# Mixing and convolution products cut from half-array to eighth-array tiles

## The reference, cut to what matters

```python
# layer 0: a 64x64 mixing matrix for each batch
agg_w = jnp.einsum('bk,koi->boi', att, weight[..., 0])
out = jnp.einsum('boi,bih->boh', agg_w, x) + agg_b[:, :, None]
# layer 1: a grouped convolution, 9 taps, 4 groups of 16 channels
out = lax.conv_general_dilated(x, weight, window_strides=(STRIDE,), padding=[(PAD, PAD)],
                               dimension_numbers=('NCH', 'OIH', 'NCH'), feature_group_count=GROUPS)
# behind both: base linear map 1024 -> 1024, and a gated low-rank part of 8 experts, rank 16
```

## Time and profile before

| | |
|---|---|
| time, median of 3 runs | 2087.89 us (2087.43 to 2088.1) |
| time of the profiled execution | 2088.04 us |
| span of the profiled execution | 2086.2 us |
| instructions in the trace | 61022 |
| granted TensorE clock, mean | 1.00 |
| PE matmuls and weight loads | 22221 of each |

### The profile page before, as it was taken

The page is one execution under the profiler, slowest core; times in us unless marked ns, Lnnn a source line. Parts: engine busy times, 40 slices in busy tenths (PEclk is TensorE's granted clock), DMA queues, the critical chain, the costliest instruction groups (busy, mean ns, idle before and its releaser), DMA issues.

```text
span 2086.2 us, 61022 instructions
## 1 busy us (share of the span) xinstructions
PE 2077.8 (100%) x22221; PEld 1979.4 (95%) x22221; DVE 1531.9 (73%) x5264; ACT 314.3 (15%) x941; POOL 966.9 (46%) x1318
## 2 busy tenths in 40 slices
PE   9999999999999999999999999999999999999999
PEld 8999999999999999999999999999999999999998
DVE  6766766667667666666788887777778888877776
ACT  4211111111111111111211111111111111111110
POOL 3644444444444444444854444444444454544442
PEclk9999999999999999999999999999999999999999
DMA  6434334343343343344433343333333333333332
GB/s 244 137 96 115 106 104 112 98 110 110 94 114 106 101 115 98 109 111 116 128 95 104 107 104 94 94 94 94 94 101 104 103 100 94 94 94 94 98 104 80
DMA packets 152180, 222.76 MB, mean 107 GB/s; under 512 B 18256, under 2 KB 100176, under 8 KB 152144
## 3 DMA queue, kind: packets, MB, share of 16 engines
q1 hardware_dynamic: 151808, 221.97, 38.9%
q10 hardware_dynamic: 336, 0.30, 0.1%
HBM read 121.47 MB, written 100.73 MB: 107 GB/s over the span
## 4 chain that ended last, share of the span: by engine, by line
PE 99%; DVE 0%; DMA 0%; ACT 0%; issue 0%; DVEq 0%; ACTq 0%
PE psB L1083 79%; PE psB L1109 8%; PE psT L1061 7%; PE psT L1024 3%; PE psB L1183 1%; DMA outb<-in_condw 0%; PE psT L1039 0%; PE psT L1117 0%; DVE Wlo L769 0%; DVE Ylo L755 0%; PE psB L1117 0%; DVE outb L804 0%; ACT Whi L572 0%; DVE Y L725 0%; DVE outb L797 0%
## 5 line engine op out<-in xcount | busy, mean ns | idle before, releaser
L1083 PE MATMUL psB<-Whi,Yhi 128*128 128x384 f32 x3024 | 723.2, 346 | 1.6 <-DVE outb L804 1.4
L1083 PE MATMUL psB<-Wlo,Yhi 128*128 128x384 f32 x3024 | 703.3, 340 | 0.0
L1083 PE MATMUL psB<-Whi,Ylo 128*128 128x384 f32 x3024 | 701.1, 339 | 0.0
L1083 PEld LDWEIGHTS psB<-Whi,Yhi 128*128 128x128 f32 x3024 | 537.7, 189 | 26.6 <-issue 2.2
L1083 PEld LDWEIGHTS psB<-Whi,Ylo 128*128 128x128 f32 x3024 | 549.8, 189 | 0.0
L1083 PEld LDWEIGHTS psB<-Wlo,Yhi 128*128 128x128 f32 x3024 | 548.6, 188 | 0.1
L442 POOL TENSOR_TENSOR res<-res,bias 128x256 f32<-128x256 f32 x256 | 180.0, 734 | 541.1 <-DMA res<-x_scratch 541.1
L917 DVE STREAM_TRANSPOSE HT<-hw 32x32 f32<-32x32 f32 x1968 | 397.5, 202 | 25.1
L471 POOL TENSOR_TENSOR Ylo<-Y,Yhi 128x256 fp32r<-128x256 f32 x244 | 190.7, 801 | 322.2 <-ACT Yhi L546 322.2
L432 POOL TENSOR_TENSOR res<-Xraw,bias 128x256 f32<-128x256 f32 x248 | 218.2, 913 | 206.0 <-DVE outb L804 195.3
L804 DVE TENSOR_TENSOR outb<-psB,res 128x384 f32<-128x384 f32 x381 | 223.6, 673 | 122.4 <-PE psB L1109 122.4
(11 more groups left out here) (132 smaller groups left out, 1578.4 us busy)
## 6 DMA issues: line engine op xcount, KB each, us to landing
x_scratch<-outb SPq DMA_DIRECT2D x64, 512.0 KB, 2.7
x_block_scratch<-outb SPq DMA_DIRECT2D x512, 64.0 KB, 1.9
Xraw<-x_block_scratch SPq DMA_DIRECT2D x128, 256.0 KB, 5.1
res<-x_scratch SPq DMA_DIRECT2D x64, 512.0 KB, 4.7
out<-outb SPq DMA_DIRECT2D x64, 512.0 KB, 2.9
Xraw<-in_x SPq DMA_DIRECT2D x62, 512.0 KB, 3.4
row<-row_scratch SPq DMA_DIRECT2D x126, 64.0 KB, 4.2
stage<-in_l0w SPq DMA_DIRECT2D x8, 580.5 KB, 12.8
```

The costliest lines, as they stand in the source:

```text
L1083: last = mm(psB[:, 3 * par + b, 0:cols], y, w[:, k, BANK0[b]:BANK0[b] + cols], start=(k == 0 and y is yh and w is Whi), stop=(k == KT - 1 ...
```

## The change

Each of the products is cut in two: the stationary operand is now 64 rows by 32 columns, its result goes to 32 partitions of psT, and `tile_position` names the eighth of the array (half the rows, a quarter of the columns) on which it stands. A round over m and a is eight products instead of four. The moving operand stays 64 by 64. A burst has 64 products, and since each is still two weight loads and two matmuls, 256 instructions instead of 128. SQ is 32.

```diff
@@ -1015,15 +1015,15 @@
-            def mix_squares(j, par):
+            def mix_eighths(j, par):
 
                 half = slice(0, C), slice(C, P)
                 for k in range(KT):
-                    for m in range(2):
+                    for m in range(0, P, SQ):
                         for a in range(2):
-                            last = mm(psT[half[m], a, k * C:(k + 1) * C],
-                                      x_tile(j, par)[half[a], k * P + m * C:k * P + (m + 1) * C],
-                                      M[half[a], half[a]], start=True, stop=True)
+                            last = mm(psT[m:m + SQ, a, k * C:(k + 1) * C],
+                                      x_tile(j, par)[half[a], k * P + m:k * P + m + SQ],
+                                      M[half[a], half[a]], start=True, stop=True, tile_position=(a * C, m))
                 last.then_inc(mixed, NC)
@@ -1055,11 +1055,11 @@
                 half = slice(0, C), slice(C, P)
                 for k in range(2):
                     for w in range(PRODUCTS):
-                        for m in range(2):
+                        for m in range(0, P, SQ):
                             for a in range(2):
                                 to = (k * PRODUCTS + w) * C
-                                last = mm(psT[half[m], a, to:to + C], Xs[half[a], w, 2 * i + k, half[m]],
-                                          CT[half[a], k, w, :], start=True, stop=True)
+                                last = mm(psT[m:m + SQ, a, to:to + C], Xs[half[a], w, 2 * i + k, m:m + SQ],
+                                          CT[half[a], k, w, :], start=True, stop=True, tile_position=(a * C, m))
                 last.then_inc(mixed, 2)
```

More of the change, by code:

```diff
@@ L1246, in step @@
                     if lay1 == 0 and k == MIX_AFTER:
-                        mix_squares(*after(j, par))
+                        mix_eighths(*after(j, par))
                     if lay1 == 1 and k in conv_after:
```

## The result

The kernel before took 2087.99 us (median of 4 runs, 2087.43 to 2088.89), the changed one 2152.85 (4 runs, 2151.16 to 2154.2): a ratio of 1.0309, 95% interval 1.0296 to 1.0322. I had forecast 2113, range 2086 to 2185, so the direction and the range held, but the change is 65 us where the forecast has 25.

A forecast was written before the change was run, and what follows sets the result against it. The prediction took TensorE, busy all the time, to bound the kernel. Instruction supply would add 0.133 us to each of 189 bursts, 25 us on 2088.04, giving 2113 us, range 2086 to 2185.

The forecast's parts named there:

- no gain on the array: In a burst, moving columns set the 58 ns round, so cutting the stationary operand saves no array time; sum 0.
- The exit of a burst: Entering and leaving a burst costs TensorE some time, claimed to be the same before and after the change.
- the supply of instructions becomes the bound: In bursts, the sequencer at 4.7 ns an instruction can't follow the array's 3.6; +0.133 us a burst, 25 us; chance 0.48.
- 223 instructions x 4.7, and some 0.03, that is 1.08: Burst from first weight load to last matmul: 256 instructions less 33 queued, at 4.7 ns each; 1.08 us against 0.945.
- 8 ns lag: Sequencer's delay in a burst, 30 ns against 22 in the slow stretch, read as supply of 4.7 ns an instruction.
- rival C: Bursts much slower: 7.3 ns is the sequencer's pace (+135 us) or an empty queue costs more (+95 us); chance 0.18.
- rival D: TensorE's code is loaded again in layer 1's loop, all 30 rounds; 2140 to 2300 us, chance 0.10.
- nothing else moved: Behind the bursts, VectorE's load per tile and its 0.8 us distance stay, and DMAs are as before.
- Rivals A and B: Sequencer needs 4.2 ns or less. A: no change, 2088, chance 0.17. B: shorter first weight load stays, 2083, chance 0.07.

The follow-up runs named there:

- half-array run: Against the kernel before: 16 products a burst over half the rows and all 128 columns, two side by side, 64 instructions; 2245.15 us.
- the quarters' run: The kernel before with two waits, long satisfied, put in the middle of each burst; 2088.12 us, ratio 1.0002.

## Why the prediction was right in direction and wrong in size

**Right: no gain on the array.** Moving columns set the round of the kernel before, with the weights close behind, and cutting the weights brought nothing back. The wide and the half-array run show both sides of it. The exit of a burst stays as it was (144 ns from last matmul to next weight load, 147 before).

**Right, in part: the supply of instructions becomes the bound.** Wide moving operands, with half the instructions, make 0.89 us of 1.268; the queue is found with 11 instructions ahead instead of 37 in the middle of a burst; pieces that are short against the queue's content run at full pace.

**Wrong: the term "223 instructions x 4.7, and some 0.03, that is 1.08".** It measured 1.268, so +0.323 us a burst and not +0.133. Three things in it:

- The pace. In the change it is one matmul in 10.04 ns from the 34th on (94 in 0.944 us), stops and all, where the forecast has 9.4. The even stretches are faster. I had read 4.7 ns an instruction out of an 8 ns lag, and the even stretches show 4.17 (8.33 a pair). The lag was of the right size for a wrong reason, or mixed with one. Taken alone this term was too long: 223 x 4.17 = 0.93.
- The start of supply. I let it begin with the burst, from a queue with 33 ahead. In the trace 66 instructions go at full pace, and then there is a hole: the 34th matmul starts 84 ns after the 32nd, and with 16 moving columns, where the array can't be the cause, 96 ns after it (0.164 to 0.260 us). The depth of the queue wasn't 33 everywhere, either: 37 in the quarters' run.
- The stops. In the even part a weight load comes late each 34 pairs, with 64 moving columns, and not with 16 or 32: from the 69th load to the 103rd it takes 329 ns, where 34 pairs at 8.33 are 283. The runs give 1.085, 1.098 and 1.268 us for 16, 32 and 64 columns, and 1.213 for 64 with half the weights. So of the 0.323 us a burst, 0.140 are there with 16 columns, and 0.183 only with 64: 0.064 ahead of the 34th matmul (0.324 against 0.260 us), where the array's rounds set the pace, and 0.119 behind it (94 steps in 0.944 us against 0.825). The 0.119 are a price that only shows with matmuls of full length and a queue near empty, and part of it is weight loads that aren't covered any more.

By the forecast's own line, 0.03 us and then 9.4 ns a pair, the 34th matmul is due at 0.20 us. It came at 0.324. So the beginning makes some 0.13 of the missing 0.19 us, and the 94 steps behind it the other 0.06.

The price of an empty queue was in my rival C ("an empty queue costs more than supply"), with +95 us and a chance of less than 0.18. What took place is between the forecast and this rival, which I had treated as an alternative though it is a consequence: once supply is the bound the queue is empty, and then what the queue hid comes out. That 2152.85 lies in the range is partly luck: the range went above 2137 for rival C, whose sum I didn't use, and for rival D, which didn't happen.

**Right: nothing else moved.** No wait for VectorE, DMAs as before. **Rival D fell:** ten more pieces of code were loaded, once; the loop of 1,352 instructions isn't loaded again in its 30 rounds. Rivals A and B would have needed 4.2 ns an instruction or less. The pace did come out at 4.17, and they didn't come true, because of the hole and the stops: their condition was stated for the wrong quantity.

**What stays open** is what makes the hole behind the 66th instruction and the stops each 34 pairs. The runs exclude the order of tiles, the count of columns on the array, tiles of 32 columns as such, and the place in the program (it is the same in all 189 bursts). The hole goes by count and not by time: it is ahead of the 34th weight load with 16, 32, 64 and 128 moving columns, where the load before stands at 0.134, 0.134, 0.195 and 0.355 us, though with 128 only 17 ns of it are left. It needs eight tiles in use: four at a time take instructions at the same 7 ns each as the wide operands, and don't have it. The regular stops came with 64 moving columns and not with 16 or 32. Each f32 product is two passes on one tile, which for eight tiles makes 32 instructions to fill them all, about the queue's content; whether the second passes clog the queue I only argue, and no run shows it.

## What to carry to other kernels

Before cutting a product into more tiles, ask which of its two lengths sets the round on the array, the moving columns or the weights; cutting the other one only adds instructions. Then divide the burst's time by its instructions: with 7.3 ns each this kernel's TensorE was safe, with 3.6 ns each it wasn't, and pieces of 64 instructions ran at full pace in any case, from a queue with some 33 ahead. And when a sum shows that a queue will run empty, price also what the full queue hid, weight loads ahead of their matmuls for one.

## What the runs showed of the hardware

- TensorE took up instructions in an even 8.33 ns for a weight load and a matmul when nothing else bound it (16 moving columns, 64 pairs in 0.533 us). Out of the queue, at a burst's start, it took 31 such pairs in 0.162 us.
- A round on the tiles takes 56 ns with 16 or 32 stationary columns, 58 with 64, 112 with 128, for 64 moving columns of f32.
- Matmuls on different tiles seem not to start in program order: 64 had started where four tiles could have begun 60.
- A hole follows the first 66 instructions of a burst in eighths, at the same place in each: from the 32nd matmul to the 34th it is 84 ns with 64 moving columns, 96 with 16, 109 with 32.
- The sequencer was 30 to 37 instructions ahead in quarters; in eighths 11 in the middle of a burst, and 19 at its end, 18 of them base products.
